# Attention: TensorE issues the products with the latents ahead of the score products in every step

## The reference, cut to what matters

```python
B, L, D = 2, 2048, 256;  H, HD, LD = 16, 64, 64
q_blhd = einsum('bld,dhk->blhk', x, Wq)
latent = einsum('bld,dc->blc', x, Wkv_down)
k_blhd = einsum('blc,chk->blhk', latent, Wk_up)
v_blhd = einsum('blc,chk->blhk', latent, Wv_up)
attn   = einsum('bqhd,bkhd->bhqk', q, k) / sqrt(HD)
attn   = softmax(where(causal mask, attn, -big), axis=-1)
y      = einsum('bqhd,hdo->bqo', einsum('bhqk,bkhd->bqhd', attn, v), Wout)
```

## Time and profile before

| | us |
|---|---|
| median of three runs | 2707.83 |
| the profiled execution | 2709.01 |
| its span, first to last instruction | 2707.2 |
| TensorE busy | 2547.4 (94%) |
| VectorE busy | 1947.0 (72%) |
| ScalarE busy | 1789.7 (66%) |
| GpSimd busy | 1866.1 (69%) |
| score products, first to last turn | 67.6 to 1724.6 |

### The profile page before, as it was taken

The page is one execution under the profiler, slowest core; times in us unless marked ns, Lnnn a source line. Parts: engine busy times, 40 slices in busy tenths (PEclk is TensorE's granted clock), DMA queues, the critical chain, the costliest instruction groups (busy, mean ns, idle before and its releaser), DMA issues. The chain is left out here.

```text
span 2707.2 us, 44944 instructions
## 1 busy us (share of the span) xinstructions
PE 2547.4 (94%) x12820; PEld 2133.8 (79%) x12820; DVE 1947.0 (72%) x4167; ACT 1789.7 (66%) x3908; POOL 1866.1 (69%) x1575
## 2 busy tenths in 40 slices
PE   5999999999999999999999999899989998889885
PEld 4888888888777788888888888688878887778774
DVE  7888888888977788888888888365754464754456
ACT  3888888888778788888888888533225663236552
POOL 3889989989879798899899898622443232544225
PEclk8999999999999999999999999999989998879997
DMA  3111112112111111111111011343444441324543
GB/s 76 39 43 46 44 42 48 37 28 53 38 41 32 26 27 28 29 31 30 27 31 26 23 23 26 103 147 123 135 151 136 145 154 55 97 102 156 176 158 121
DMA packets 170930, 192.97 MB, mean 71 GB/s; under 512 B 57843, under 2 KB 143225, under 8 KB 170182
## 3 DMA queue, kind: packets, MB, share of 16 engines
q1 hardware_dynamic: 157382, 156.26, 20.8%
q0 software_dynamic: 12288, 33.57, 3.7%
q10 hardware_dynamic: 1024, 0.26, 0.0%
HBM read 116.02 MB, written 83.16 MB: 74 GB/s over the span
## 5 line engine op out<-in xcount | busy, mean ns | idle before, releaser
L382 POOL TENSOR_TENSOR pl<-pr,ph 128x512 fp32r<-128x512 f32 (+1 forms) x1024 | 1300.8, 1293 | 181.6 <-ACT ph L860 164.5
L857 ACT ACTIVATE pr<-ps 128x512 f32<-128x512 f32 (+1 forms) x1152 | 664.0, 576 | 289.7 <-DVE ps L1046 145.3
L1133 DVE TENSOR_REDUCE part<-ps 128x1 f32<-128x512 f32 (+2 forms) x1152 | 697.3, 618 | 84.1 <-PE ps L571 68.2
L860 ACT ACTIVATE ph<-ps 128x512 fp32r<-128x512 f32 (+1 forms) x1152 | 664.7, 577 | 0.0
L571 PE MATMUL ps<-k_hi,q_parts 128*128 128x512 f32 (+3 forms) x1280 | 472.3, 369 | 27.3 <-DVE part L1133 10.7
L584 PE MATMUL ps<-q_parts,k_hi 128*128 128x512 f32 (+1 forms) x1152 | 443.2, 385 | 0.3 <-ACT ph L860 0.3
L585 PE MATMUL ps<-q_row,k_lo 65*128 65x512 f32 (+1 forms) x1152 | 443.4, 385 | 0.0
L571 PEld LDWEIGHTS ps<-k_hi,q_parts 128*128 128x128 f32 x1280 | 242.5, 189 | 91.6 <-DVE part L1133 19.2
L1785 PE MATMUL ps<-exp_up,yy 128*128 x888 | 250.8, 419 | 2.6 <-ACT yy L1958 2.4
L584 PEld LDWEIGHTS ps<-q_parts,k_hi 128*128 128x128 f32 x1152 | 217.2, 188 | 43.5 <-ACT ph L860 0.7
L585 PEld LDWEIGHTS ps<-q_row,k_lo 65*128 65x128 f32 x1152 | 217.1, 188 | 25.3
(11 more groups left out here) (257 smaller groups left out, 4555.1 us busy)
## 6 DMA issues: line engine op xcount, KB each, us to landing
work<-x_slots SPq DMA_DIRECT2D x148, 128.0 KB, 2.2
e_slots<-work SPq DMA_DIRECT2D x148, 128.0 KB
y_latent<-y_sums SPq DMA_DIRECT2D x128, 128.0 KB
yg<-y_latent SPq DMA_DIRECT2D x32, 512.0 KB, 5.1
rec<-recip_rows SPq DMA_DIRECT2D x127, 128.0 KB, 3.0
x_slots<-zero_rows SPq DMA_DIRECT2D x32, 296.0 KB, 3.9
acc_shared<-accw SPq DMA_DIRECT2D x14, 512.0 KB, 2.9
accr<-acc_shared SPq DMA_DIRECT2D x12, 512.0 KB, 3.7
```

Source lines behind the costliest of these rows:

```text
L382: eng.tensor_tensor(pl[:, s % RING, 0:w], pr[:, s % PR_RING, 0:w], f32(ph[:, s % RING, 0:w]), ALU.subtract).then_inc(sem, 1)
L857: act.activation(pr[:, s % PR_RING, 0:w], src, ACT.Exp).then_inc(S["probs"], 1)
L860: act.activation(ph[:, s % RING, 0:w], src, ACT.Exp).then_inc(S["probs_hi"], 1)
L1133: dve.tensor_reduce(dst, src[:, 0:w], AX.X, ALU.max).then_inc(S["max_read"], 1)
```

## The change

Before, a step is: first use of the ring (nearly always a maximum product), score products, second use of the ring, products with the latents, further uses. After, it is: first use of the ring, products with the latents, second use of the ring, score products, further uses. No other engine's list is changed, and the numbers that semaphores are compared with stay the same.

```diff
--- before.py
+++ after.py
@@ -652,13 +652,13 @@
                         uses = ring_at(s, p)
                         for use in uses[:1]:
                             fill_bank(p, *use)
-                        scores(s, p, first)
-                        for use in uses[1:2]:
-                            fill_bank(p, *use)
                         if s >= LAG:
                             use_latents(p, s - LAG)
                         elif not first:
                             use_latents(p - 1, STEPS + s - LAG)
+                        for use in uses[1:2]:
+                            fill_bank(p, *use)
+                        scores(s, p, first)
                         for use in uses[2:]:
                             fill_bank(p, *use)
```

## The result

The changed kernel took 2763.97 us in the median of four runs (2757.86 to 2768.8), beside 2708.76 for the kernel before on the same chip. The ratio is 1.0199, with a 95% interval of 1.0178 to 1.0221: 55 us slower. The forecast was 2747, so the direction was right and the loss was 38 us instead of 55.

What follows compares the result with a forecast made beforehand. TensorE's instruction list was taken as the bound, busy 102.14 of 102.35 us in turn 3. Waits of 32.5 + 1.6 + 2.8 + 1.9 = 38.8 us on 2709.0 gave 2747.8, forecast as 2747, range 2724 to 2780.

Steps and rivals of the forecast that it cites:

- (a): Latent products at step 52 of ordinary turns wait for GpSimd's remainder of step 47: 0.87 us a turn.
- (b): Maximum product at step 36, already waiting for VectorE's reduction of its bank, waits 0.64 us longer a turn.
- (c): Step 9, already waiting on a chain from a mask that waited for scores: 0.36 us more a turn.
- (d): Maximum product at step 1 waits for reductions behind a mask that waited for scores: 0.33 us a turn.
- (e): Steps 12 and 23, ring waits behind late masks: 0.13 and 0.16, together 0.29 us a turn.
- The rival that parts the two engines at step 52: GpSimd and VectorE no longer contend there, returning 0.49 us in each of 13 turns: 2741 us, chance 0.08.
- the sign named for step 36: A ring wait of about 1 us at step 36 would show the forecast right.
- both go back to S: At step 52 the GpSimd and VectorE chains both start from the score products (S) and move by the same 0.71 us.
- Turns 6 and 7: Turn 6: four VectorE chains from late masks, 2.8 us; turn 7: a latent product's 1.17 and a ring wait's 0.7, 1.9.
- "proj" jobs: Jobs ScalarE reads, 2.1 us less slack where they now stand ahead of scores; taken as 0, at most 0.3 a turn.
- turn 15: No queries to split for a successor, so the step 52 wait is gone: 1.6 us.

Runs made afterwards that it cites:

- a9: Changed order in steps 42 to 52 alone, the other steps as in the kernel before: ratio 1.0039 to the kernel before, 2723.5 us.
- a8: Changed kernel, but diagonal steps keep the old order: ratio 1.0055 to the kernel before, 2727.6 us.
- a4: Changed kernel with VectorE reading the step's maxima before it adds the mask in diagonal steps: ratio 1.0120 to the kernel before, 2742.4 us.
- a10: Kernel before plus a small memset on GpSimd ahead of the remainder of step 30, turns 9 to 14 only: ratio 0.9993, 2708.9 us.
- a1: Kernel before with only the second ring use moved, behind the products with the latents: ratio 0.9948, 2699.6 us.
- a12: Order maximum, scores, latents, second use, but latents ahead of the maximum in step 0 of turns 7 and 8: ratio 0.9969 to the kernel before, 2702.2 us.
- a7: Kernel before plus a reduction of a constant mask on VectorE behind the mask of step 28, all turns but the sixth: ratio 1.0001, 2709.6 us.

## Why the prediction was right, and where it was off

By the steps of the forecast, for an ordinary turn (from the distances in turn 3, after less before):

| step of the forecast | forecast | measured |
|---|---|---|
| (a) latent products at step 52 | 0.87 | 0.78, and 0.25 at ring waits of steps 50 and 51 |
| (b) maximum product at step 36 | 0.64 | -0.50 |
| (c) step 9 | 0.36 | 0.37, and 0.19 at step 7 |
| (d) start of the turn | 0.33 | 0.89 (steps 0 to 2) |
| (e) steps 12 and 23 | 0.29 | 0.52 (steps 12, 13, 22 to 24) |
| steps 42, 43 and 57 | none | 0.51 |
| sum | 2.5 | 3.0 |

**Right.** The mechanism: nothing is added, scores come 0.71 us later and latent products 0.46 earlier, and the cost is what the slack doesn't cover. (a) alone is shown by a9, the masks' part by a8 and a4. The rival that parts the two engines at step 52 did not come true: GpSimd's instruction there took 1.75 us after and 1.78 before.

**The size was partly luck.** (b) was expected at +0.64 and came at -0.50. Without it the forecast had 1.85 us for a turn, and the runs show 3.5. Two errors of opposite sign left a sum near the measured one. Of the sign named for step 36, a wait of about 1 us, nothing came.

**(b) had the wrong sign.** The forecast carried the shift of 0.70 through VectorE's chain as if its instructions kept their durations. They don't: this chain has an instruction that takes 0.68 or 1.68 us by when GpSimd starts its own. a10 shows it. The forecast weighed the rule of the Trainium skill (GPSIMD Engine Reference, Specifications) that the two engines contend when VectorE's instruction has two SBUF inputs. It did so at step 52, found that both chains move alike, and left it out. It is step 32 where it mattered: there a shift of 0.15 us between the two engines (from 0.16 behind to 0.01) was enough, and "both go back to S" doesn't rule that out.

**(d) was put at the wrong instruction.** I looked at the slack of maximum products alone. The ring is also used by row jobs, and the one at step 0 reuses the bank that the late reduction frees. The one at step 57 is the same case (0.31).

**(e) was mis-sized.** A maximum product that waits also delays the weight load behind it: a wait of 0.12 to 0.15 at the ring has 0.07 to 0.10 behind it, in the gap to the next product. Five such pairs, at steps 2, 12, 22, 42 and 50, come to 1.1 us of the turn. The 0.19 at step 7, beside (c), is another sort: a latent product that starts a block, and by the times it waits for ScalarE's copy of a finished one (the copy ends at 390.88, the product starts at 391.03).

**Turns 6 and 7 were mis-sized most.** Forecast 2.8 and 1.9, measured 5.2 and 7.9. At the end of turn 6 the wait for the ring grew by 0.94, near the 0.7 that the forecast counted there, but the clock then fell, 2.9 us, and the same in turn 8. That is less than half of turn 7's 7.9. Most of the rest is ring waits, which the forecast had at one 0.7: they are new at steps 21 (1.3) and 57 (0.8), and grew by 0.7 at step 48 and by 0.94 at the turn's end. The one at step 21 stands three uses of the ring behind a "lat" job, whose six products now come ahead of the step's score products; the forecast reckoned with such a shift for the "proj" jobs alone. The latent products for which it counted 1.17 cost 0.3 less than before. I took the ordinary turns' granted clock of 1.00 for all, though the kernel before has the same thing in turn 6 behind a wait of 4.2 us. The Trainium skill (TensorE: Matmul & The Clock Gate, section "HAM oscillation — how this bites in real kernels") warns of idle gaps for this reason; the trace agrees that the clock falls behind a gap. The gaps in the page's example are longer than those here, and the measurement decides: it fell behind a wait of 1.7 us (a1), and stayed at 1.00 behind one of 2.5 us (a4).

**The account.** Of the 19.6 us between the forecast sum (38.8) and the profile (58.4), the ordinary turns have 6.3 (2.9 of it is turn 8's clock), turns 6 and 7 8.4, turn 15 1.9 (the last products wait 2.0 us for VectorE's remainder of 4.97 us, where I had counted ring waits alone), and the stages ahead of and behind the attention 3.0, which no step of the forecast touches and which is within their variation. So about 8 us, the two falls of the clock and the long remainder, are outside the forecast's mechanism.

## What to carry to other kernels

When an in-order engine is full and its groups are reordered, the price is a ledger: for each wait, how long its result had been ready, less how much nearer the new order brings producer and consumer. List the slack of *every* user of a shared buffer ring, not only of the kind that is in view. Check two things the ledger leaves out: instructions on two engines of which one holds up the other by which starts first, and waits behind which TensorE's clock falls.

## What the runs showed that I had not expected

- Two remainders of the same shape, one on VectorE (0.68 us alone) and one on GpSimd (1.29 alone): which starts first decides which is held up. Where VectorE began behind GpSimd, it ended about 1.84 us after GpSimd had begun, for distances up to 1 us: in the kernel before it took 1.78 us when 0.06 behind, 1.68 when 0.16, 1.43 when 0.41, 1.24 when 0.61 and 0.89 when 0.95. Where the two began within 0.01 us or VectorE was ahead, VectorE took 0.68 to 0.83 and GpSimd 1.83 (together) to 1.36 (0.49 behind).
- Behind a series of GpSimd remainders without a pause, VectorE's can wait for more than one of them. At the end of turn 15 it took 4.97 us in the changed kernel and 5.43 and 5.39 in a1 and a12, in each over four GpSimd instructions, and 1.65 in the kernel before, where GpSimd's series also ran without a pause. What made the difference stays open.
- Because the order of the starts decides, 0.52 us of useless work on GpSimd made a turn 0.6 us shorter (a10), and moving one ring use behind the latent products made the kernel 0.5% faster (a1), for a reason that has little to do with the ring.
- The reverse hid an experiment: 0.68 us of added work on VectorE was given back by a cast that took 0.95 instead of 1.47 us (a7).
- A wait of 2.68 us of TensorE cost 2.9 us more in the 6 us behind it, at a granted clock of 0.50; a wait of 1.74 at the same place cost nothing more. Elsewhere the clock fell behind a wait of 1.7 us and not behind one of 2.5: the length of the wait doesn't decide it alone.
